# A recurrent block and an attention block on one core: preparing the weights beside the first chunk, fewer waits, single-pass bias rows, another order

## The chip, the cores and the metric

One NeuronCore of a Trainium2 chip runs the whole program. The metric is the device time of one execution in microseconds. The five engines are TensorE (PE), VectorE (DVE), ScalarE (ACT), GpSimd (POOL) and SyncE (SP), which here only issues transfers.

## What is computed

x is [2, 2048, 256] in float32 (2 sequences, 2048 positions, width 256). Two layers follow each other, each `x = x + s(xn) * silu(g(xn))` with `xn = layernorm(x)`:

```
layer 0: s = mamba block (in_proj 256->2x512, 4-tap causal conv, silu, dt = softplus(...),
             state scan h = exp(dt*A)*h + dt*B*x over 2048 positions, 512 channels x 16 states,
             y = sum_n h*C + D*x, gated by silu(z), out_proj) then layernorm and ffn 256->1024->256
         g = fp4_linear(silu(fp4_linear(x, w_gate)) * fp4_linear(x, w_up), w_down)   # blocks of 16, 704 wide
layer 1: s = attention over the 2 sequences at each position (16 heads of 16), with in and out projection
         g = three residual blocks of two 4-bit linears (weight q/7.5-1 times a scale per 16, plus
             a rank-32 part lora_b @ lora_a, plus bias) with layernorm and gelu between
```

The FP4 linears quantize both sides: `scale = max|block|/6`, rounding to the grid 0, 0.5, ... 6, and back.

## The kernel before, in words

The 2048 positions go in 16 chunks of 128 positions (TC) of both sequences. Everything is float32. One period of a software pipeline handles one chunk's state scan and, for chunks before and after it, the other steps. The steps have names, and each engine has its order of steps written out by hand (`PE_PLAN`, `ACT_PLAN`, `POOL_PLAN`, `DVE_PLAN`, `SP_PLAN`); a `+` or `-` behind a name says how many chunks ahead or behind the period's own chunk the step works. The engines meet only at semaphores, `at(name, chunk, k)`. PE's results outside the scan go through three PSUM banks in turn, in PE's own order (`BANK`, `EARLIER`): a step waits until the bank's user three steps before has been read.

The state scan goes by state n = 0..15 in two halves (a, b) of 4 x 128 columns: ACT's `exp` (L742) writes the decays into one of three PSUM tiles `unit`; POOL's `drive` (L965) multiplies wx = dt*x by the row B, broadcast to all partitions by a transfer `rows` of SP, and L971 adds the carry from the chunk before; DVE's `scan` (L1127), then `hc` (L1133), times the row C, then `clr` (L1140); ACT's `out` (L750) saves the carry; PE's `sum` (L537) transposes and adds hc into `y_ps`.

The front of a chunk is: DVE `f` (statistics), POOL `f`, ACT `xn`, `xhf`, PE `uT`, ACT `u`, PE `xi0..3` and `z0`, `z1`, ACT `tap0..3`, DVE `conv0`, `conv1`, ACT `xc0`, `xc1`, PE `xp` (L575), SP `wr` (rows B and C to DRAM), PE and ACT `dt0`, `dt1`, ACT `dtexp` (L813), `dtln`, POOL `log` (L1013), DVE `dt` (L1166), `wx` (L1170). POOL's `arg` and `fix0` make the first column's carry.

Six linears of a period end in a bias row (`bias_row`, L516): b0a, b1a, b2a, q and ao over 512 columns, v1 over 256. It is a product of a column of the identity, broadcast, with the six rows of `b_rows`.

Before this loop a block of its own prepares the weights, with memory that is given back afterwards. SP issues 34 loads on one semaphore, and PE, ACT, DVE and POOL wait for all of them. DVE (L196 to L202) finds the scales of the gate, up and down weights, POOL divides (L311), DVE rounds in four steps (L334 to L341), POOL multiplies back (L314), one weight after the other. DVE dequantizes the 4-bit weights (L343, L347). PE then makes 26 groups of transposes (L384), copied by ACT (L369), through three banks, and 12 folds (L396, L398): two products with the identity that turn a 4-bit weight and one that adds the low-rank part; ACT copies each (L372). The loop's block starts after all engines have left this one.

## Time and profile before

| | us |
|---|---|
| median of 3 runs | 1854.18 (1853.78 to 1857.8) |
| the profiled execution's own time | 1856.52 |
| its span, first to last instruction | 1854.7 |
| mean granted TensorE clock, share of full | 0.953 |
| PE, DVE, ACT, POOL busy | 1577.4, 1551.4, 1437.5, 1252.4 |

The profile is of one execution. Busy is the time in which an engine has an instruction running; an idle engine is only a loss where it is what the end waits for. Times in the rows are in microseconds from the first instruction, mean durations in ns.

### The profile page before, as it was taken

Reading aid. Unit: us, or ns where it says so; the run is one execution under the profiler, and the core shown is the slowest. Engines: PE = TensorE matmul, PEld = TensorE weight load, DVE = VectorE, ACT = ScalarE, POOL = GpSimd, SP = SyncE. Lnnn points to the kernel's source line nnn. Section 1 sums busy time; section 2 is a strip of 40 time slices with the busy share of each in tenths; the row PEclk is TensorE's granted clock in tenths of the full one; section 3 lists DMA queues with packets and bytes.
Section 4 is the critical chain, followed back from the end, with each engine's and each line's share of the span. In section 5 each row is a group of like instructions: output and inputs, shape, how many; then the busy total and the mean of one; then the engine's idle time right before and its main releaser. Section 6 shows DMA issues by size and latency. Waiting matters only on the chain.

```text
span 1854.7 us, 28175 instructions
## 1 busy us (share of the span) xinstructions
PE 1577.4 (85%) x7632; PEld 1164.4 (63%) x7632; DVE 1551.4 (84%) x2882; ACT 1437.5 (78%) x3076; POOL 1252.4 (68%) x1313
## 2 busy tenths in 40 slices
PE   0083768899999999999989999999989999999875
PEld 0051556586767677776767676767667767767653
DVE  0623999999999999999999999999999999999811
ACT  0034678898989898989889888989888989888723
POOL 0304676777777786868687777778686868787522
PEclk9976789999999999999999999999999999999987
DMA  8000111111111111111111111111111211111100
GB/s 209 0 6 29 52 47 58 47 57 37 58 48 60 43 52 51 59 47 52 52 52 52 44 51 50 58 47 46 58 52 47 63 41 58 46 44 55 35 0 12
DMA packets 68395, 91.70 MB, mean 49 GB/s; under 512 B 15674, under 2 KB 34686, under 8 KB 68238
## 3 DMA queue, kind: packets, MB, share of 16 engines
q1 hardware_dynamic: 68238, 89.91, 15.8%
q8 instruction: 62, 1.02, 0.2%
q14 instruction: 95, 0.78, 0.1%
HBM read 85.17 MB, written 4.72 MB: 48 GB/s over the span
## 4 chain that ended last, share of the span: by engine, by line
PE 27%; POOL 20%; DVE 16%; issue 16%; ACT 12%; POOLq 0%; ACTq 0%; DVEq 0%; DMA 0%
PE bank L511 10%; POOL drive L965 10%; PE bank L627 6%; DVE unit L1127 4%; DVE hc L1133 3%; PE bank L516 2%; PE y_ps L537 2%; ACT unit L742 2%; PE bank L498 1%; PE bank L563 1%; ACT op_a L709 1%; DVE xc L1158 1%; ACT L709 1%; ACT L923 1%; POOL s L1068 1%
## 5 line engine op out<-in xcount | busy, mean ns | idle before, releaser
L965 POOL TENSOR_TENSOR drive<-wx,rows 128x1024 f32<-128x1024 f32 x256 | 604.1, 2360 | 163.3 <-DVE unit L1127 82.8
L1127 DVE TENSOR_TENSOR_SCAN unit<-unit,drive 128x512 f32<-128x512 f32 x512 | 616.7, 1221 | 30.7 <-POOL drive L971 23.4
L742 ACT ACTIVATE unit<-dt,aneg 128x254 f32<-128x254 f32 x1024 | 441.9, 468 | 19.8 <-ACT carry L750 0.7
L1133 DVE TENSOR_TENSOR hc<-unit,rows 128x512 f32<-128x512 f32 x512 | 340.9, 684 | 8.8 <-issue 3.0
L537 PE MATMUL y_ps<-ident,hc 128*128 128x128 f32 x2048 | 278.1, 282 | 52.5 <-DVE hc L1133 52.4
L537 PEld LDWEIGHTS y_ps<-ident,hc 128*128 128x128 f32 x2048 | 241.2, 145 | 115.3 <-DVE hc L1133 71.8
L742 ACT ACT_TABLE_LOAD x109 | 139.8, 1283 | 3.7
L750 ACT ACTIVATE carry<-unit 128x4 f32<-128x4 f32 x512 | 79.3, 169 | 66.8 <-DVE unit L1140 63.0
L627 PE MATMUL bank<-op_a,w_f 128*128 128x256 f32 x512 | 115.7, 385 | 11.2 <-ACT op_a L709 11.2
L709 ACT ACT_TABLE_LOAD x77 | 98.8, 1283 | 22.4 <-PE bank L498 21.6
L511 PE MATMUL bank<-w_f,wide 128*128 128x256 f32 x512 | 113.3, 379 | 1.5 <-ACT wide L709 1.5
L627 PEld LDWEIGHTS bank<-op_a,w_f 128*128 128x128 f32 x512 | 97.0, 192 | 27.1 <-ACT op_a L709 11.9
L511 PE MATMUL bank<-w_d,hq_t 128*128 128x256 f32 (+1 forms) x384 | 109.3, 436 | 0.0
L511 PEld LDWEIGHTS bank<-w_f,wide 128*128 128x128 f32 x512 | 96.0, 190 | 14.9 <-ACT wide L709 1.7
L516 PE MATMUL bank<-b_rows,ident 6*128 6x512 f32 (+1 forms) x192 | 100.9, 605 | 0.0
L511 PEld LDWEIGHTS bank<-w_d,hq_t 128*128 128x128 f32 (+1 forms) x384 | 78.6, 219 | 27.0 <-issue 16.4
L593 PE MATMUL bank<-w_g,xq_t 128*128 128x352 f32 x256 | 87.3, 464 | 5.0 <-ACT xq_t L821 5.0
L1013 POOL TENSOR_SCALAR wide<-wx 128x1024 f32<-128x1024 f32 x16 | 58.4, 3652 | 46.8 <-ACT wx L813 46.8
L384 PE MATMUL bank<-ident,gate_raw 88*128 88x88 f32 x32 | 4.9, 355 | 97.2 <-POOL down_raw L314 97.2
L593 PE MATMUL bank<-w_u,xq_t 128*128 128x352 f32 x256 | 84.0, 460 | 1.3 <-ACT hq L827 1.1
L1038 POOL TENSOR_TENSOR hq<-q,j_scl 128x704 f32<-128x704 f32 x32 | 44.4, 1387 | 54.1 <-DVE q L1114 54.1
L722 ACT ACTIVATE xht<-bank,b_sm 128x256 f32<-128x256 f32 x96 | 48.7, 558 | 38.2 <-POOL b_sm L953 38.2
(220 smaller groups left out, 3439.4 us busy)
## 6 DMA issues: line engine op xcount, KB each, us to landing
rows<-rows_scratch SPq DMA_DIRECT2D x256, 256.0 KB, 3.3
x_t<-in_L_attn_x_dram SPq DMA_DIRECT2D x16, 256.0 KB, 3.7
x<-in_L_attn_x_dram SPq DMA_DIRECT2D x16, 256.0 KB, 3.3
out_dram<-x SPq DMA_DIRECT2D x16, 256.0 KB, 2.1
w_f<-in_L_attn_ffn_w_dram SPq DMA_DIRECT2D x2, 1024.0 KB
q_raw<-in_L_ffn_qweights_dram SPq DMA_DIRECT2D x1, 1536.0 KB
w_in<-in_L_attn_in_proj_w_dram SPq DMA_DIRECT2D x1, 1024.0 KB
qkv_raw<-attn_in_proj_weight_dram SPq DMA_DIRECT2D x1, 768.0 KB
```

What stands on the lines that cost most here:

```text
L511: last = t.matmul(dst[:, j * D:(j + 1) * D], lhs(k, j), rhs(k), start=(k == 0 and j == 0), stop=(stop and k == kp - 1), skip_group_check=True)
L516: return t.matmul(dst[:, 0:wide_ * D], ident[0:NROW, row:row + 1].to_broadcast([NROW, P]), b_rows[:, None, :].to_broadcast([NROW, wide_, D ...
L537: last = t.matmul(y_ps[j][:, g * P:(g + 1) * P], hc[n % NPROD][:, g * B + j, :], ident[:, :], start=False, stop=(n == NS - 1), is_transpos ...
L593: last = t.matmul(dst[:, 0:IH], xq_t[:, k, j, :], wt[:, k, half * IH:(half + 1) * IH], start=(k == 0), stop=(k == KD - 1))
L627: last = t.matmul(dst[:, a * TOK:(a + 1) * TOK], w_f1[:, k, (2 * m + a) * P:(2 * m + a + 1) * P], op_a[:, k, :], start=(k == 0 and a == 0) ...
L709: last = a_.activation(dst(k), src[:, k * TOK:(k + 1) * TOK], func, scale=scale(k), bias=bias(k))
L742: last = a_.activation(u[:, k * TOK:(k + 1) * TOK].rearrange("p (b t) -> p b t", b=B)[:, :, 1:TC], dt[p][:, g, :].rearrange("p (b t) -> p ...
L750: a_.activation(carry[:, n, 4 * half:4 * half + 4], unit_of(ch, n, half)[:, :].rearrange("p (s t) -> p s t", t=TC)[:, :, TC - 1], ACT.Copy)\
L965: g_.tensor_tensor(drive[n % 2][:, :, :].rearrange("p (g b) t -> p g b t", b=B), wx[p][:, :, :].rearrange("p g (b t) -> p g b t", b=B), ro ...
L1013: g_.tensor_scalar(tmp_u, wx[p][:, :, :], 1.0, -1.0, ALU.add, ALU.add).then_inc(S["sp_pool"], 1)
L1127: v.tensor_tensor_scan(u[:, :], u[:, :], d, 0.0, ALU.mult, ALU.add).then_inc(S["scan_done"], 1)
L1133: v.tensor_tensor(hc[n % NPROD][:, 4 * half:4 * half + 4, :].rearrange("p (g b) t -> p g b t", b=B), unit_of(ch, n, half)[:, :].rearrange( ...
```

## The change

1. Preparation and front together. The separate block is gone. In one block each engine does the front of chunk 0 (`FRONT`) between its preparation steps, and the loop leaves those steps out (`due`). Loads have four semaphores: `front_in`, `gate_in`, `lora_in`, `rest_in`. Raw weights lie in tiles that the loop uses later (drive, hc, rows, ops, xs, hx, hq), which is why those tiles are now allocated together. The groups of transposes and the folds use the two `y_ps` tiles in turn, not three banks, in the order low-rank, folds, rest, gate, down. The identity products of a fold are marked `is_transpose`.
2. Waits. `exp` waits for dt_ready, `out` and `drive` for carry_in, `drive` for wx_ready and `scan` for drive_ready only where the value first matters; `hc` b no longer waits for y_summed, `hc` no longer for its rows.
3. Bias rows. `b_rows` is loaded twice, at partitions 0 and 32. `b_two` holds the value rounded to float32r at 0 and what rounding left at 32; `pick` is two 32 x 32 identities. The bias row is one product of 64 partitions in float32r.
4. Order. The five plans have the same steps in another order. The period's boundary is moved, so some steps carry another offset (z1, sum7, aexp, v1, out10b, dt1, dtexp, hc15b and most of SP's); no step is added or dropped.

```diff
 ACT_PLAN = """
-    exp12a- hq1- hq2- out11a- exp12b- out11b- h1-- exp13a- ctx-- out12a- out12b- exp13b- out13a- exp14a- exp14b-
-    usave dtln gatec--- out13b- exp15a- out14a- exp15b- first out14b- exp0a b1n-- gatem- b1g-- out15a- exp0b
-    out15b- s1-- yg0- xq exp1a out0a out0b exp1b yg1- exp2a out1a exp2b g00 out1b g01 exp3a out2a exp3b g10
...
+    aexp-- dt1 out10b- v1-- dtexp out11a- exp12a- exp12b- h1-- hq1- out11b- ctx-- exp13a- dtln out12a- exp13b-
+    usave out12b- exp14a- out13a- out13b- hq2- first exp14b- out14a- exp15a- exp15b- b1n-- out14b- exp0a
+    gatec--- out15a- gatem- b1g-- exp0b s1-- out15b- xq exp1a yg0- yg1- out0a exp1b out0b exp2a out1a exp2b g00
...
 SP_PLAN = """
-    rows8- rows11- load+ rows10- rows12- rows13- wr rows14- rows15- rows0 rows1 rows3 rows2 store--- rows4
-    again- rows6 rows5 rows9 rows7
+    wr- rows0- rows15-- rows14-- rows2- rows1- rows3- rows4- store---- rows5- rows7- rows6- rows9- again--
+    rows8- rows10- load+ rows12- rows11- rows13-
 """
+FRONT = {
+    "SP": ("load", "wr"),
+    "POOL": ("f", "log"),
+    "ACT": ("xn", "xhf", "u", "tap0", "tap1", "z0", "tap2", "tap3", "z1", "xc0", "xc1", "usave", "xp", "dt0", "dt1",
+            "dtexp", "dtln"),
+    "PE": ("uT", "xi0", "xi1", "z0", "xi2", "xi3", "z1", "xp", "dt0", "dt1"),
+    "DVE": ("f", "conv0", "conv1", "dt", "wx"),
+}
             def bias_row(dst, row, wide_):
-                return t.matmul(dst[:, 0:wide_ * D], ident[0:NROW, row:row + 1].to_broadcast([NROW, P]),
-                                b_rows[:, None, :].to_broadcast([NROW, wide_, D]), start=False, stop=True,
+                return t.matmul(dst[:, 0:wide_ * D], pick[:, row:row + 1].to_broadcast([2 * LOW, P]),
+                                b_two[:, None, :].to_broadcast([2 * LOW, wide_, D]), start=False, stop=True,
                                 skip_group_check=True)
...
-                dve.wait_ge(*at("drive_ready", ch, 2 * n + 2))
+                if half == 0:
+                    dve.wait_ge(*at("drive_ready", ch, 2 * n + 2))
                 dve.wait_ge(*at("decay_ready", ch, 2 * n + half + 1))
...
+                    sp_step(sp, "load", 0)
+                    for dst, src in load_front:
+                        sp.dma_start(dst, src).then_inc(front_in, 16)
+                    for dst, src in load_gate:
+                        sp.dma_start(dst, src).then_inc(gate_in, 16)
+                    for dst, src in load_lora:
+                        sp.dma_start(dst, src).then_inc(lora_in, 16)
+                    for dst, src in load_rest:
+                        sp.dma_start(dst, src).then_inc(rest_in, 16)
+                sp_step(sp, "wr", 0)
+                sp.wait_ge(w_rounded, 4 * len(weights))
+                sp.wait_ge(turn_out, N_LB + N_FOLD)
...
+                pool_step(pool, "f", 0)
+                divide(0)
+                divide(1)
+                unscale(0)
+                divide(2)
+                unscale(1)
+                pool_step(pool, "log", 0)
+                unscale(2)
+                pool.wait_ge(rest_in, 16 * len(load_rest))
+                pool.wait_ge(turn_out, N_TURNS - IK)
...
+                act.wait_ge(front_in, 16 * len(load_front))
+                for name in FRONT["ACT"][:FRONT["ACT"].index("xp")]:
+                    act_step(act, name, 0)
+                nc.scalar.activation(aneg[:, :, :], al_raw[:, :, :], ACT.Exp).then_inc(neg_exp, 1)
+                for n, (dst, parts) in enumerate(lb_turns):
+                    turn_copy(dst, parts, n)
+                for name in FRONT["ACT"][FRONT["ACT"].index("xp"):]:
+                    act_step(act, name, 0)
...
+                pe.wait_ge(lora_deq, 2)
+                pe.wait_ge(turn_out, N_LB)
+                for n, (i, k) in enumerate(folds):
+                    m = N_LB + n
+                    pe.wait_ge(turn_out, m - 1)
+                    dst = y_ps[m % 2]
+                    for j in range(KD):
+                        nc.tensor.matmul(dst[:, j * P:(j + 1) * P], l_raw[:, i * KD + j, k * P:(k + 1) * P],
+                                         ident[:, :], start=(j == 0), stop=False, is_transpose=True, skip_group_check=True)
...
+                pe.wait_ge(w_out_done, 3)
+                for n, (dst, parts) in enumerate(gate_turns):
+                    turn_in(parts, N_LB + N_FOLD + N_REST + n)
+                pe.wait_ge(turn_out, N_TURNS)
...
+                dve_step(dve, "f", 0)
+                dve.wait_ge(gate_in, 16 * len(load_gate))
+                scale(0)
+                scale(1)
+                dve_step(dve, "conv0", 0)
+                step_of(0)
+                dve_step(dve, "conv1", 0)
+                round_(0)
+                scale(2)
+                step_of(1)
+                round_(1)
+                dve.wait_ge(lora_in, 16 * len(load_lora))
...
+                step_of(2)
+                round_(2)
+                dve_step(dve, "dt", 0)
+                dve_step(dve, "wx", 0)
...
+                dve.wait_ge(turn_out, N_TURNS - IK)
```

`scale` is the four instructions L196 to L202, `step_of` the first two and `round_` the last two of the rounding, `divide` and `unscale` POOL's two products. `load_front` holds w_in and nine transfers of columns and of the dt and B/C weights, `load_gate` three, `load_lora` four, `load_rest` the other 21.

## Rows read from the trace of the kernel before

**Rows 1.** The page: busy time by engine, and the row loads' time to landing.
```profile
PE 1577.4 (85%) x7632; PEld 1164.4 (63%) x7632; DVE 1551.4 (84%) x2882; ACT 1437.5 (78%) x3076; POOL 1252.4 (68%) x1313
...
rows<-rows_scratch SPq DMA_DIRECT2D x256, 256.0 KB, 3.3
```
**Rows 2.** Windows: length, busy time of each engine, granted clock, DMA share, GB/s.
```profile
0.00:10.00 10.00, 0.00 (x0) 0.00 (x0) 0.00 (x0) 1.28 (x1) 0.80 (x9) 1.00 0.87 274
10.00:20.00 10.00, 0.00 (x0) 0.00 (x0) 0.00 (x0) 0.00 (x0) 0.00 (x0) 1.00 0.80 162
45.00:100.30 55.30, 3.07 (x21) 3.10 (x22) 36.47 (x26) 2.10 (x5) 21.30 (x6) 1.00 0.00 0
...
109.40:136.00 26.60, 25.48 (x72) 15.79 (x72) 0.12 (x3) 4.61 (x12) 0.25 (x2) 0.55 0.00 1
...
400.00:500.00 100.00, 93.72 (x472) 69.26 (x470) 94.74 (x182) 89.33 (x192) 76.83 (x81) 1.00 0.15 51
900.00:1000.00 100.00, 93.72 (x471) 69.28 (x470) 94.32 (x179) 89.27 (x192) 76.86 (x81) 1.00 0.17 52
```
**Rows 3.** Timeline of the preparation: start, length, engine, line, operation.
```profile
45.27 2.28 DVE L196 TENSOR_REDUCE q_amax<-gate_raw 88x128 f32<-88x2048 f32 x1 [45.27 <-DMA lb_raw<-in_L_ffn_lora_b_dram]
...
49.20 3.67 POOL L311 TENSOR_TENSOR gate_raw<-gate_raw,q_rcp 88x2048 f32<-88x2048 f32 x1 [47.64 <-DVE q_rcp L202]
...
55.42 2.29 DVE L339 TENSOR_TENSOR gate_raw<-gate_raw,qt 88x2048 f32<-88x2048 f32 x1
...
94.68 5.62 DVE L347 TENSOR_TENSOR l_raw<-l_raw,sc_raw 128x3072 f32<-128x3072 f32 x1
...
99.26 0.46 ACT L369 ACTIVATE w_g<-bank 128x352 f32<-128x352 f32 x1
...
110.68 0.71 PE L396 MATMUL bank<-ident,l_raw 128*128 128x128 f32 x4
...
127.95 1.22 PE L396 MATMUL bank<-ident,l_raw 128*128 128x128 f32 x4
...
130.25 1.22 PE L396 MATMUL bank<-ident,l_raw 128*128 128x128 f32 x4
...
134.96 0.38 ACT L372 ACTIVATE w_l<-bank 128x256 f32<-128x256 f32 x1 [1.92 <-PE bank L398]
```
**Rows 4.** Timeline of chunk 0's front, to the first drive.
```profile
156.72 1.27 DVE L1158 SCALAR_TENSOR_TENSOR xc<-bank,cw,xc 128x256 f32<-128x256 f32 x3 [0.41 <-ACT xc L776]
...
168.69 3.64 POOL L1013 TENSOR_SCALAR wide<-wx 128x1024 f32<-128x1024 f32 x1 [21.65 <-ACT wx L813]
...
177.28 1.23 DVE L1166 TENSOR_TENSOR dt<-wide 128x1024 f32<-128x1024 f32 x1 [17.56 <-POOL wide L1018]
...
181.11 2.79 POOL L965 TENSOR_TENSOR drive<-wx,rows 128x1024 f32<-128x1024 f32 x1
```
**Rows 5.** The chain of waits over one period: start, length, what.
```profile
912.15 0.70 DVE s L1205
...
934.50 1.05 PE bank L516 x2
935.54 0.60 PE bank L498 x4
...
1000.61 1.05 PE bank L516 x2
...
1011.79 0.70 DVE s L1205
```
**Rows 6.** Groups by line, 912.15 to 1011.79: busy us, mean ns, idle before.
```profile
L1127 DVE TENSOR_TENSOR_SCAN unit<-unit,drive 128x512 f32<-128x512 f32 x32 | 38.5, 1221 | 1.9 <-POOL drive L971 1.7
L965 POOL TENSOR_TENSOR drive<-wx,rows 128x1024 f32<-128x1024 f32 x16 | 37.7, 2358 | 9.1 <-DMA rows<-rows_scratch 6.2 <-DVE unit L1127 2.9
...
L742 ACT ACT_TABLE_LOAD x7 | 9.0, 1283 | 0.2
...
L516 PE MATMUL bank<-b_rows,ident 6*128 6x512 f32 (+1 forms) x12 | 6.3, 603 | 0.0
```
**Rows 7.** The chain of waits in the tail.
```profile
1744.42 1.06 PE bank L516 x2
...
1755.06 0.44 PE bank L498 x4
```

More of the change, by code:

```diff
@@ L37 @@
 XW = NTAP - 1 + TC
+LOW = 32
 MAGIC = 1.5 * 2 ** 22
@@ L114, with due @@
 PERIODS = range(-6, NC + 6)
+FRONT = {
[6 more added lines that the diff above has]
+}
 def there(chunk):
     return 0 <= chunk < NC
-ORDER = [(_c + _o, _n) for _c in PERIODS for _n, _o in plan(PE_PLAN) if _n in USE and there(_c + _o)]
+def due(engine, name, chunk):
+    return there(chunk) and not (chunk == 0 and name in FRONT[engine])
+ORDER = [(0, _n) for _n in FRONT["PE"]]
+ORDER += [(_c + _o, _n) for _c in PERIODS for _n, _o in plan(PE_PLAN) if _n in USE and due("PE", _n, _c + _o)]
 BANK = {_key: _k % NBANK for _k, _key in enumerate(ORDER)}
@@ new lines, in program @@
+        folds = [(i, k) for i in range(NLIN) for k in range(KD)]
+        N_LB, N_FOLD, N_REST, N_GATE = len(lb_turns), len(folds), len(rest_turns), len(gate_turns)
+        N_TURNS = N_LB + N_FOLD + N_REST + N_GATE
+        weights = [(gate_raw[0].rearrange("p j (s b) -> p (j s) b", b=QB), GR, NGP * D // QB),
+                   (gate_raw[1].rearrange("p j (s b) -> p (j s) b", b=QB), GR, NGP * D // QB),
+                   (down_raw[:, :, :].rearrange("p k (s b) -> p (k s) b", b=QB), P, KD * IQ // QB)]
@@ L1276, in program, with pieces @@
+        def pieces(n):
+            rows_, nb = weights[n][1:]
+            return [small[n][0:rows_, 128 * i:128 * i + nb] for i in range(3)]
         with nc.Block() as block:
@@ L1313, in _, with scale, wait @@
             def _(dve):
-                for k in range(NUNIT):
-                    nc.vector.memset(unit[k][:, :].rearrange("p (s t) -> p s t", t=TC)[:, :, 0], 0.0).then_inc(c_prep, 1)
-                dve.wait_ge(c_prep, 6 * 3 + 3 + DG + NUNIT)
+                v = nc.vector
+                def scale(n):
+                    src, rows_, nb = weights[n]
+                    amax_, scl_, rcp_ = pieces(n)
+                    k = [4 * n]
+                    def wait():
+                        k[0] += 1
+                        dve.wait_ge(w_scaled, k[0])
+                    fp4_dve_scale(v, src, rows_, nb, amax_, scl_, rcp_, (w_scaled, 1), wait)
@@ L1318, in _ @@
+                for g in range(DG):
+                    v.tensor_scalar(d_diag[:, g, :], ident[:, :], dsk[:, g:g + 1], None, ALU.mult).then_inc(small_done, 1)
+                dve.wait_ge(turn_out, N_TURNS - IK)
                 for c in PERIODS:
                     for name, off in plan(DVE_PLAN):
-                        if there(c + off):
+                        if due("DVE", name, c + off):
                             dve_step(dve, name, c + off)
```

445 lines of the change are left out of this document (219 added, 226 removed).

## Prediction

> **What bounds the kernel now.** The page first: PE and DVE are both busy for over four fifths of the span, ACT and POOL for less [rows 1]. The windows then tell where the idle part is. Head: up to 45 us only loads run; from 45 to 100.3 the weights pass through DVE and POOL in turns, 36.5 us of DVE work in 55.3 us, with PE and ACT almost idle; then PE and ACT turn the weights and fold the low-rank parts until 136 [rows 2]. Only then is the first chunk of x loaded. Middle: a period is 99.64 us from one chunk's addition at L1205 to the next [rows 5], and in 100 us PE is busy for 93.7, DVE for 94.3, ACT for 89.3 and POOL for 76.9 [rows 2]. PE and DVE have some 6 us to spare, and the chain of waits changes engine all the time (it is on PE at 934.50 and 1000.61, on DVE at 912.15 [rows 5]), so what leaves one engine comes back only in part. Tail: behind the last chunk's scans, from about 1711 us, the chain of waits is mostly PE's [rows 7].
>
> The timeline of the head gives the anchors. All engines start at 45.27, when the last of all loads has landed; the dequantized low-rank weights are ready at 100.3; the second fold starts at 110.68, and the last fold's copy at 134.96 [rows 3]; x is asked for behind it. The front of chunk 0 then takes until 177.28 for dt, and the first drive, with which the state loop starts, is at 181.11 [rows 4]. This last is the head's length; what changes it shifts everything behind it by as much.
>
> **The head, part by part.** The load order is new: x and the ten transfers that the front needs, then the gate weights (2.1 MB), low-rank, rest. Up to the gate weights these are about 3.6 MB. The first 10 us moved 274 GB/s and the next ten 162, as there the small vector transfers are issued [rows 2]; 3.6 MB take 13 us by the first and 22 by the second. I take 18, since the six vector and column transfers of the front lie before the gate's. The upper bound for a mixing of the transfers is 33 us (15 more).
>
> DVE then sets the pace, because its order is one queue: statistics, then a wait for the gate weights, and behind that wait conv0. PE's xi2 needs the bank that conv0 frees, so the whole front is held until this wait ends; that costs the front some 10 us, but DVE is needed for the weights anyway. Up to the second dequantization step DVE has all of the 36.5 us [rows 2] less the last weight's stepping and rounding (1408 columns; by the 2.29 us of an addition of 2048 columns [rows 3] some 1.6 us each for two operations and, an estimate, half of that for the other two: 5 us), so 31.5, plus 5.1 us for conv0 and conv1 (12 steps, three in 1.27 us [rows 4]): 36.7 us. I add 2.5 us for conv1 waiting on PE and ACT. Dequantized at 18 + 36.7 + 2.5 = 57 us, where it was 100.3. DVE and POOL no longer alternate, since four waits on POOL (3.67 us each for the 2048 columns [rows 3]) lie beside other DVE work; if that cover were gone, the 14.7 us would return.
>
> POOL carries the divisions, the unscalings and log(1+.): 21.3 us [rows 2] plus 8.6 (log starts at 168.69 and lets dt go at 177.28 [rows 4]). It has log behind unscale(1), which waits for DVE's rounding at about 50 us, so log ends near 63 and dt near 65. Folds and turns end later than that, so it costs nothing.
>
> The folds wait for the dequantization. Before, each takes 2.30 us from start to start at the low clock (127.95 to 130.25), and its first half, four records for two identity products, 1.22 us there and 0.71 at the high clock [rows 3]. Marked as transposes they are two records, as the four transposes of a step are four records, in 0.60 us [rows 5]. I take 1.8 us: 12 x 1.8 = 21.6 us, end at 79; at the high clock, by 0.71 to 1.22, 12 x 1.05 puts it at 70. The clock stood at 0.55 on the mean in that stretch [rows 2] although PE hardly paused, so I take the low one. Then 6 turns of q/k/v and output weights and 8 of gate and up weights, on two PSUM tiles in place of three. A copy takes 0.46 us [rows 3]; with its hand-over, the clock low and one tile fewer I take 0.7: 14 x 0.7 = 9.8, end at 89. There POOL and DVE are let go, DVE has the scale of x (1.5 us), POOL its product; ACT has six more copies of w_down (3.6 us), then exp of the first column, then fix0. Drive0 at about 95.5. SP is held until the folds end, 79, and its row loads land in 3.3 us [rows 1], before the drives. The head thus goes from 181.1 to 95.5: **-85.6 us**; bounds 84 (high clock) and 110 (late loads), so -97 to -71.
>
> **The bias rows.** A period has 12 records at L516, 6.3 us of PE [rows 6]: five products of 512 columns and one of 256, two records each. On the chain a wide one costs 1.05 us [rows 5]. The trace of before has no float32r product. The nearest row is that of one-record products, the transposes: four of 128 columns, together 512, take 0.60 us on the chain [rows 5], 0.44 at best [rows 7]. Bounds: 0.44 from there, and 1.05 for no gain, by which 23.5 us of the sum below would be lost. The product is one record like theirs, so I take 0.44, a gain of 0.6. By the Trainium skill ("FP8 and Floating Point Precision", TensorE Precision Notes) true float32 is four passes through the array and reduced float32 one; an estimate from that page is 0.26 us for a wide row, a gain of 0.79, and no run shows it yet. In the period shown two wide rows lie on the chain, at 934.50 and at 1000.61 [rows 5]: 2 x 0.6 = **-1.2 us a period, 15 periods: -18 us**. In the tail the chain has nine of them, the first at 1744.42 [rows 7]: 9 x 0.6 = **-5.5 us**.
>
> **Leaner waits.** Per period they drop a wait from 31 exponentials, 30 carries, 29 drive steps, 16 scans and 48 in hc. DVE's idle time before scans is 1.9 us, of which 1.7 are for POOL's drive [rows 6], and that wait remains. The other 0.2 us, and as much again on hc and the carries, bound the gain at some 0.5 us a period, 7 us in all; a loss is excluded, as nothing is added. I take 0.
>
> **The order.** Steps and distances are nearly the same; aexp, v1, out10b, dt1, dtexp, z1 and sum7 cross the period's boundary only because it was moved, as do most of SP's. Counting changes of function around ACT_PLAN gives 20 table loads where the old plan has 19, at 1.28 us (seven of them are at L742 [rows 6]): +1.28 us on ACT, which goes from 89 to 90 busy and still has slack. SP's order changes which row load stands behind which hc wait; POOL waited 6.2 us a period for rows and 2.9 for scans [rows 6], and as POOL has 23 us to spare a shift of some us there is hidden. Net 0, from -2.3 us (DVE loses 3.5 of its 5.6 idle us, 1.2 of them counted already) to +2.5 us a period (the table load and as much again on the chain).
>
> **Sum**, against the profiled execution's own 1856.5: -85.6 - 18 - 5.5 = 1747.4. The median of the runs is 2.3 us lower, so **1745 us**.
>
> **Rivals.** (a) *PE's relief lets the period shrink.* DVE sets the floor at 94.0 us busy, and with some 3 us less PE work its waits on PE and on drives go too: 2.3 us a period more than summed, 35 us, 1710 us. For it: PE and DVE are both full. Against: the chain has ACT and POOL pieces as well. (b) *The order costs.* An extra table load on the chain plus as much waiting, 2.5 us x 15 = 37: 1782 us. For it: ACT is 89% busy already. (c) *Late loads.* Transfers issued later share the engines with the gate's, DVE starts 15 us later: 1760 us. For it: the 162 GB/s of 10 to 20 us. (d) *The other side: the clock.* With less PE work per period the granted clock, 1.00 in the middle windows [rows 2], falls to 1.2 GHz for part of each. Half a fold costs 1.22 against 0.71 us at the two levels [rows 3], so PE's 90 us become 90 x (1 + 0.7 s) for a share s. Head and tail give 91 us, 6.1 a period, so it decides from a period of 105.7, s = 0.25; at a third it would be 111 us and the kernel at 1854 - 91 + 15 x 11.4 = 1934. Against it: PE still idles only in pieces of a few us. The Trainium skill ("TensorE: Matmul & The Clock Gate", What's actually happening) has the throttled state as the default which activity releases; by that rule PE's lighter period would invite it. The trace agrees only in part: in the folds PE was busy for 25.5 of 26.6 us and the clock stood at 0.55 [rows 2]. (e) *The preparation stays serial:* DVE's wait for the gate weights holds the front and gains vanish. The sum of DVE work above speaks against it; even 30 us more leaves 1775.
>
> **Chances and range.** Forecast (1725 to 1765) 0.52; (a) 0.17; (b) 0.12; (c) and a mild (e), 1760 to 1775, 0.14; (d) 0.03; the rest 0.02. No more than 2 in 10 left out: 1707 to 1778. Faster 0.96, within 0.2% 0.01, slower 0.03; 0.2% is about what a measurement of this kernel can tell from none.
>
> **What would show it.** In the profile after: drive0 at 84 to 110 us; DVE's first reduce near 18; folds starting after 57, two transpose records and 1.8 us each; L516's successor with one record per row and under 0.6 us; the period between additions at L1205's successor 98.4 us; 20 table loads. The prediction is wrong if the dequantization ends after 75 us, or if the period moves by over 2 us either way.

## The result

The changed kernel takes 1798.52 us (median of 4 runs, 1796.36 to 1800.92), the kernel before 1855.99 beside it: ratio 0.9689, 95% interval 0.9668 to 0.9711. It is 3.1% faster, where the forecast of 1745 was 5.9% and the range ended at 1778.

The page of the profile after: its busy line, its clock line and two groups (line, engine, operation | busy us, mean ns | idle before):
```profile
PE 1568.4 (87%) x7512; PEld 1162.3 (65%) x7512; DVE 1556.0 (87%) x2887; ACT 1449.5 (81%) x3091; POOL 1246.3 (69%) x1314
...
PEclk8567898999999999999999998989999999999888
...
L959 DVE TENSOR_TENSOR_SCAN unit<-unit,drive 128x512 f32<-128x512 f32 x512 | 616.7, 1221 | 47.0 <-ACT unit L570 37.8
...
L579 ACT ACTIVATE carry<-unit 128x4 f32<-128x4 f32 x512 | 83.1, 169 | 138.3 <-DVE unit L973 137.8
```
The same two groups on the page of before:
```profile
L1127 DVE TENSOR_TENSOR_SCAN unit<-unit,drive 128x512 f32<-128x512 f32 x512 | 616.7, 1221 | 30.7 <-POOL drive L971 23.4 <-ACT unit L742 4.6 <-issue 0.2
...
L750 ACT ACTIVATE carry<-unit 128x4 f32<-128x4 f32 x512 | 79.3, 169 | 66.8 <-DVE unit L1140 63.0
```
DVE's busy time is 5 us above that of before [rows 1], with 60 us less span. What is new is in the idle column: scans (L959) wait for ACT's exponentials (L570) where they waited for POOL's drives, and ACT's carry copies (L579) stand 138 us waiting for DVE's clears (L973) where they stood 66.8.

I cut both spans at the first drive and at the first and the fifteenth addition of a chunk. The mark of an addition is L1205 before and L1038 after, the product with the gate just ahead of it:

| us | first drive | first addition | 14 periods | after them | span |
|---|---|---|---|---|---|
| before | 181.11 | 315.37 | 1393.42 | 145.91 | 1854.7 |
| after | 109.97 | 244.18 | 1411.46 | 138.86 | 1794.5 |
| change | -71.1 | -71.2 | **+18.0** | -7.1 | -60.2 |

The forecast had -85.6, then -16.8 (14 x 1.2), then -6.7 (the tail's 5.5 and the last period's 1.2). So 14 us are missing in the head and 35 in the middle. The windows of the 14 periods, after:
```profile
244.18:1655.64 1411.46, 1312.51 (x6452) 982.70 (x6451) 1309.61 (x2486) 1249.85 (x2666) 1060.74 (x1122) 0.96 0.16 50
```
and before:
```profile
315.37:1708.79 1393.42, 1317.75 (x6540) 977.09 (x6539) 1314.80 (x2484) 1238.09 (x2650) 1071.19 (x1123) 0.99 0.16 51
```
DVE has 5 us less work in them than before and ACT 12 more, so for DVE the periods grew by idle time. PE is busy for 5 us less only, although its bias rows alone went from 88.1 to 40.5 us in these periods: its other work takes 42 us more, at a granted clock of 0.96 for 0.99.

The head, timeline after, DVE (start, length, line, operation [idle before]):
```profile
28.20 2.28 DVE L217 TENSOR_REDUCE ctx<-drive 88x128 f32<-88x2048 f32 x1 [17.43 <-DMA hq<-in_L_ffn_w_down_dram]
30.52 0.22 DVE L219 TENSOR_SCALAR ctx<-ctx 88x128 f32<-88x128 f32 x1
...
34.21 1.61 DVE L219 TENSOR_SCALAR s<-s 88x128 f32<-88x128 f32 x1
...
56.10 3.49 DVE L1367 TENSOR_SCALAR rows<-rows 88x2048 f32<-88x2048 f32 x1
...
65.94 6.72 DVE L1395 TENSOR_TENSOR ops<-ops,v 128x3072 f32<-128x3072 f32 x1
...
82.88 3.53 DVE L999 TENSOR_TENSOR dt<-wide 128x1024 f32<-128x1024 f32 x1 [2.30 <-POOL wide L849]
...
104.28 0.69 DVE L217 TENSOR_REDUCE x_amax<-xn 128x32 f32<-128x512 f32 x1 [14.24 <-ACT w_u L1274]
```
and the queue of SP, PE and POOL in the same stretch:
```profile
6.83 0.44 SPq L1099 DMA_DIRECT2D x_t<-in_L_attn_x_dram  x1
...
72.71 0.69 PE L1325 MATMUL y_ps<-ident,ops 128*128 128x128 f32 x2 [15.11 <-DVE ops L1395]
73.33 1.22 PE L1327 MATMUL y_ps<-hx,xs 32*128 32x256 f32 x2
74.48 0.69 PE L1325 MATMUL y_ps<-ident,ops 128*128 128x128 f32 x2
...
93.92 3.02 PE L1306 MATMUL y_ps<-ident,hq_t 128*128 128x128 f32 x12
...
109.97 2.34 POOL L795 TENSOR_TENSOR drive<-wx,rows 128x1024 f32<-128x1024 f32 x1
```

| us | gate weights in | dequantized | folds end | turns end | first drive |
|---|---|---|---|---|---|
| forecast | 18 | 57 | 79 | 89 | 95.5 |
| measured | 28.2 | 72.7 | 93.9 | 104.3 | 110.0 |

All of the gap is there when the folds start: 10.2 us because the gate weights come later, the rest because DVE takes 44.5 us where I had 39.2. Behind that each stage is within 1 us of its term: 12 folds at 1.77 us, at the low clock (0.50), for 1.8. Windows over the folds, after:
```profile
72.00:94.00 22.00, 21.29 (x49) 9.52 (x50) 15.44 (x17) 4.22 (x11) 13.16 (x4) 0.50 0.00 1
```

The bias row, on the chain of waits after (start, length, what): a wide row at the high clock, a row of 256 columns at the high clock, and a wide row at the low clock.
```profile
803.72 0.42 PE bank L343
...
875.69 0.32 PE bank L343
...
1747.41 0.72 PE bank L343
```
A wide row at the high clock is one record of 0.42 to 0.44 us for 1.05 [rows 5]; the forecast took 0.44.

### The profile page after: what moved, and what is told of

Read it like the earlier page. It is cut to its first block, busy times and chain, and to the rows that moved or that the text cites. A ratio compares the mean times of both kernels' runs of the same rounds, so it can differ in the third digit from the quotient of the medians.

```text
span 1794.5 us, 26244 instructions
## 1 busy us (share of the span) xinstructions
PE 1568.4 (87%) x7512; PEld 1162.3 (65%) x7512; DVE 1556.0 (87%) x2887; ACT 1449.5 (81%) x3091; POOL 1246.3 (69%) x1314
## 4 chain that ended last, share of the span: by engine, by line
PE 46%; ACT 20%; DVE 14%; issue 12%; POOL 4%; DMA 2%; SPq 1%; POOLq 0%; ACTq 0%; DVEq 0%
PE bank L338 20%; PE bank L420 7%; PE bank L454 6%; DVE unit L959 5%; ACT unit L570 5%; PE y_ps L364 5%; PE bank L325 2%; DVE hc L966 2%; ACT L536 2%; POOL drive L795 2%; ACT L617 2%; ACT L570 2%; PE bank L343 1%; ACT ops L536 1%; PE bank L390 1%
## 5 line engine op out<-in xcount | busy, mean ns | idle before, releaser
L959 DVE TENSOR_TENSOR_SCAN unit<-unit,drive 128x512 f32<-128x512 f32 x512 | 616.7, 1221 | 47.0 <-ACT unit L570 37.8
L570 ACT ACTIVATE unit<-dt,aneg 128x254 f32<-128x254 f32 x1024 | 437.7, 467 | 7.7
L338 PE MATMUL bank<-w_l,ops 128*128 128x256 f32 x768 | 193.2, 396 | 20.2 <-ACT ops L536 18.6
L579 ACT ACTIVATE carry<-unit 128x4 f32<-128x4 f32 x512 | 83.1, 169 | 138.3 <-DVE unit L973 137.8
L338 PEld LDWEIGHTS bank<-w_l,ops 128*128 128x128 f32 x768 | 145.1, 196 | 60.4 <-issue 30.7
L338 PE MATMUL bank<-w_d,hq_t 128*128 128x256 f32 (+1 forms) x384 | 130.4, 500 | 23.4 <-ACT hq_t L668 23.4
L338 PEld LDWEIGHTS bank<-w_d,hq_t 128*128 128x128 f32 (+1 forms) x384 | 89.6, 248 | 62.6 <-ACT hq_t L668 24.9
L454 PE MATMUL bank<-ops,w_f 128*128 128x256 f32 x512 | 120.1, 388 | 2.3 <-DVE hq L1016 1.7
L338 PE MATMUL bank<-w_f,wide 128*128 128x256 f32 x512 | 113.3, 379 | 0.1
L536 ACT ACT_TABLE_LOAD x77 | 98.8, 1283 | 15.2 <-PE bank L325 14.0
L454 PEld LDWEIGHTS bank<-ops,w_f 128*128 128x128 f32 x512 | 94.9, 192 | 23.1 <-ACT ops L532 5.4
L338 PEld LDWEIGHTS bank<-w_f,wide 128*128 128x128 f32 x512 | 96.0, 190 | 12.9 <-ACT wide L536 0.3
L325 PE MATMUL bank<-ident,hx 128*128 128x128 f32 x448 | 68.5, 282 | 28.8 <-ACT hx L549 17.6
L390 PE MATMUL bank<-u_t,w_in 128*128 128x262 f32 x256 | 74.0, 417 | 16.1 <-DVE xc L994 11.7
L844 POOL TENSOR_SCALAR wide<-wx 128x1024 f32<-128x1024 f32 x16 | 62.9, 3934 | 35.9 <-ACT wx L642 35.9
```

The costliest lines, as they stand in the source:

```text
L325: last = t.transpose(dst[0:rows, n * P:(n + 1) * P], src, ident[:, :])
L338: last = t.matmul(dst[:, j * D:(j + 1) * D], lhs(k, j), rhs(k), start=(k == 0 and j == 0), stop=(stop and k == kp - 1), skip_group_check=True)
L390: last = t.matmul(dst[:, 0:B * XW], w_in[:, k, g * P:(g + 1) * P], u_t[:, k, :, :], start=(k == 0), stop=(k == KD - 1))
L454: last = t.matmul(dst[:, a * TOK:(a + 1) * TOK], w_f1[:, k, (2 * m + a) * P:(2 * m + a + 1) * P], op_a[:, k, :], start=(k == 0 and a == 0) ...
L536: last = a_.activation(dst(k), src[:, k * TOK:(k + 1) * TOK], func, scale=scale(k), bias=bias(k))
L570: last = a_.activation(u[:, k * TOK:(k + 1) * TOK].rearrange("p (b t) -> p b t", b=B)[:, :, 1:TC], dt[p][:, g, :].rearrange("p (b t) -> p ...
```

## The experiments

The kernels were timed in groups on several chips (after; e1 to e4; e5 to e8; e9 to e12; e13 to e16; e17 and e18), and those of a group share their runs of the kernel before. Ratios are to it, and differences between kernels are taken from the ratios, times 1856 us. The median of the kernel before moved from 1847.8 to 1856.0 us between the groups (in one of them its runs go from 1845.9 to 1864.2), so a difference across groups can be off by some us more than its intervals say. The columns "14 periods" and "first drive" are from each one's profile, and the clock is the mean granted in those periods.

| | ratio (95%) | median us | first drive | 14 periods, clock |
|---|---|---|---|---|
| before | 1 | 1855.99 | 181.1 | 1393.4, 0.99 |
| after | 0.9689 (0.9668 to 0.9711) | 1798.5 | 110.0 | 1411.5, 0.96 |
| e1_order_old | 0.9574 (0.9551 to 0.9597) | 1770.2 | 108.1 | 1386.3, 0.98 |
| e2_bias_old | 0.9806 (0.9784 to 0.9828) | 1814.2 | | 1418.1, 0.99 |
| e3_waits_old | 0.9766 (0.9741 to 0.9791) | 1807.4 | | 1417.9, 0.96 |
| e4_head_only | 0.9657 (0.9637 to 0.9677) | 1784.4 | 109.8 | 1393.5, 0.99 |
| e5_b_order_new | 1.0142 (1.0116 to 1.0168) | 1882.7 | 171.1 | 1431.9, 0.97 |
| e6_b_bias_new | 0.9911 (0.9888 to 0.9935) | 1838.7 | 171.8 | 1390.3, 0.98 |
| e7_load_now | 0.9684 (0.9658 to 0.9711) | 1795.5 | 104.5 | 1413.3, 0.96 |
| e8_b_waits_new | 1.0014 (0.9993 to 1.0034) | 1858.1 | 170.7 | 1393.8, 0.99 |
| e9_old_order_load_now | **0.9523 (0.9495 to 0.9550)** | 1765.5 | 102.8 | 1384.6, 0.99 |
| e10_hq2_early | 0.9684 (0.9656 to 0.9712) | 1795.7 | | 1407.8, 0.98 |
| e11_act_plan_old | 1.0434 (1.0401 to 1.0467) | 1934.3 | | 1535.7, 0.93 |
| e12_pe_plan_new | 0.9987 (0.9965 to 1.0009) | 1851.6 | | 1466.0, 0.99 |
| e13_one_silu_visit | 0.9903 (0.9875 to 0.9930) | 1833.0 | | 1444.7, 0.95 |
| e14_down_product_first | 0.9707 (0.9685 to 0.9729) | 1797.0 | | 1411.7, 0.96 |
| e15_both | 0.9920 (0.9895 to 0.9945) | 1836.3 | | 1442.5, 0.95 |
| e16_old_order_down_first | 0.9530 (0.9509 to 0.9552) | 1765.7 | | 1385.5, 0.97 |
| e17_exp_first | 0.9655 (0.9629 to 0.9681) | 1789.1 | 110.0 | 1407.9, 0.97 |
| e18_pool_products_cut | 0.9473 (0.9449 to 0.9496) | 1757.1 | 94.2 | 1383.6, 0.99 |

### The four parts, one by one

e1, e2 and e3 are the changed kernel with one part put back: the five plans (e1), the bias rows (e2), the waits (e3). e4 is the kernel before with the new head alone. e5, e6 and e8 are the kernel before with one part alone: the plans, the bias rows, the waits. The edits are the parts of the diff; for e2:
```diff
-                return t.matmul(dst[:, 0:wide_ * D], pick[:, row:row + 1].to_broadcast([2 * LOW, P]),
-                                b_two[:, None, :].to_broadcast([2 * LOW, wide_, D]), start=False, stop=True,
+                return t.matmul(dst[:, 0:wide_ * D], ident[0:NROW, row:row + 1].to_broadcast([NROW, P]),
+                                b_rows[0:NROW, None, :].to_broadcast([NROW, wide_, D]), start=False, stop=True,
```


> The changed kernel with the five plans of before (head, waits and bias rows stay new). Between the additions of the first and the 15th chunk the kernel before took 1393.4 us, the changed one 1411.5. Theory A, the new order costs: PE stands before the down product for hq2, its clock falls to the low level, and the long chain of PE work behind it runs slow. Then with the old order this stretch is 1375 to 1394 us, the whole about 1765 to 1780 us against 1798.5, and the granted clock in the middle windows is back at 0.98 to 1.00. Theory B, the cheaper bias rows leave PE less active and so the clock falls: then the stretch stays at 1405 to 1412 us, the clock at 0.95, the whole at 1790 to 1800.

> The changed kernel with the float32 bias rows of before (two records each, 1.05 us for a wide one on the chain, against 0.43 now). Theory A (order): the chain of the new order is PE's for more than half of a period, so dearer rows cost: 0.6 us for each of two to five rows a period, 18 to 45 us, 1816 to 1840 us. Theory B (activity): the clock returns to 0.98 or more and the whole falls to 1780 to 1790 us. If the rows are off the chain: within 4 us of 1798.5.

> The changed kernel with all waits of the state loop as before. My prediction gave the leaner waits 0 us, at most 0.5 us a period (7 us in all): 1798 to 1806 us. The rival, that each wait costs its engine some 50 ns of issue where instructions are short (154 waits a period over three engines), would give 2 us a period and more: 1830 us.

> The changed kernel with order, waits and bias rows of before: only the preparation beside the front is new. The head was 71.1 us shorter to the first drive, the tail's gain is the bias rows'. If the parts add up: 1856 - 71 = 1785 us, the stretch between the first and the 15th addition 1393 us. If the new head also disturbs the middle (its phase of the clock, the different tiles in memory), the stretch is longer than 1398 us.

> The kernel before with only the five new plans. Theory A (the order costs by itself): 1856 plus the stretch's 18 us plus what the float32 bias rows cost in the new order's PE chain, 1874 to 1900 us, the clock in the middle at 0.95 to 0.97. Theory C, the new order only pays together with the cheap bias rows and leaner waits it was made for: slower by the same, but then bias rows alone on the old order gain less than 10 us. If the order is neutral: 1850 to 1862.

> The kernel before with only the new bias rows. The prediction's own term: two wide rows on the chain a period, 1.2 us x 15 = 18 us, and 5.5 in the tail: 1832 us. If PE has slack there in the old order and DVE sets the pace: only the tail's 5 to 7 us, 1849. If PE's lighter period lets the clock fall (the rival of the prediction): slower than 1856.

> The kernel before with only the leaner waits. By the prediction 0 to 7 us of 1856; by the rival of 50 ns a wait some 30 us. Its middle stretch of 1393 us shows it, as nothing else differs.

**Head.** e4 is 64 us under the kernel before, and its periods have the length they had before. The profiles say 71 because in the profiled execution of before the first drive was at 181.1; in e5, e6 and e8, whose head is that of before, it was at 171.1, 171.8 and 170.7. The folds make the difference: in those three they ran at the high clock and took 14.6 us, in the profile of before 24.3 us at 0.55. Windows of e6:
```profile
110.00:124.00 14.00, 13.67 (x66) 8.95 (x66) 0.00 (x0) 4.02 (x11) 0.00 (x0) 1.00 0.01 1
```
With the new head they stood at 0.50 in all 16 profiled executions. Whether that comes from their marking as transposes or from PE's wait ahead of them (15.11 us in after, 0.55 before) no run tells apart.

**Bias rows.** Alone they take off 0.0089, 16.5 us (e6); from e4 to e1 it is 15.4 us, waits included, and from e2 to after 21.7, all within their intervals of each other. The forecast had 23.5. e6 came out between its two expectations, 1832 and 1849.

**Waits.** On the old order nothing (e8, +0.1%, the interval holds 1). On the new order with the new bias rows putting the waits back costs 14 us (e3; by the two intervals 8 to 20, by the medians 9), more than the 7 us that I had as the most. On the new order with the old bias rows they seem worth nothing: e5 less the head's gain (e4) gives 0.9799, and e2, which has the lean waits besides, 0.9806. So the gain isn't secured, and which wait it is I can't name.

**Order.** It costs: e1 is 21 us under after (15 to 27), and the new order alone adds 26 us to the kernel before (e5, 22 to 31). Two routes and one answer; by the medians it is 28 and 29.

Where it costs, one period each of e2 (new order) and e4 (old order), which differ in the order and in the waits and have the same bias rows. Groups by line, 850.99 to 952.52 of e2:
```profile
L959 DVE TENSOR_TENSOR_SCAN unit<-unit,drive 128x512 f32<-128x512 f32 x32 | 38.6, 1220 | 2.5 <-ACT unit L570 2.3
...
L579 ACT ACTIVATE carry<-unit 128x4 f32<-128x4 f32 x32 | 5.1, 167 | 7.4 <-DVE unit L973 7.4
...
L1028 DVE TENSOR_TENSOR sz<-y_ps,sz 128x512 f32<-128x512 f32 x2 | 1.3, 686 | 1.1 <-PE y_ps L364 1.1
...
L1038 DVE TENSOR_TENSOR s<-bank,ops 128x512 f32<-128x512 f32 x1 | 0.7, 691 | 0.9 <-PE bank L356 0.9
```
and 841.06 to 940.95 of e4:
```profile
L954 DVE TENSOR_TENSOR_SCAN unit<-unit,drive 128x512 f32<-128x512 f32 x32 | 38.6, 1221 | 1.9 <-POOL drive L798 1.7
...
L577 ACT ACTIVATE carry<-unit 128x4 f32<-128x4 f32 x32 | 4.9, 168 | 2.5 <-DVE unit L967 2.3
...
L1022 DVE TENSOR_TENSOR sz<-y_ps,sz 128x512 f32<-128x512 f32 x2 | 1.3, 682 | 0.0
```
The work is the same. In the new order the scans wait for exponentials instead of drives, the additions wait for PE (1.1 and 0.9 us), and ACT waits three times as long in front of carry copies. Two such waits, timeline of ACT in e2:
```profile
892.84 0.17 ACT L579 ACTIVATE carry<-unit 128x4 f32<-128x4 f32 x1 [0.22 <-DVE unit L973]
895.79 0.17 ACT L579 ACTIVATE carry<-unit 128x4 f32<-128x4 f32 x1 [2.78 <-DVE unit L973]
...
896.62 0.85 ACT L570 ACTIVATE unit<-dt,aneg 128x254 f32<-128x254 f32 x2
898.94 0.17 ACT L579 ACTIVATE carry<-unit 128x4 f32<-128x4 f32 x1 [1.47 <-DVE unit L973]
```
ACT stands for 2.8 us on clear 13b, which DVE does behind the product dt, and exponential 14b is queued behind it. These rows show where engines stand; which of the waits costs time is for the next runs.

### Is it one plan, or one place in a plan?

e11 is the changed kernel with the old ACT_PLAN alone, e12 is e9 with the new PE_PLAN alone.

> The changed kernel with only ACT_PLAN of before. It has 19 table loads a period instead of 20, and hq2 right behind hq1. If the loss sits in ACT's order (the extra load of 1.28 us and hq2): ratio 0.957 to 0.962, as with all five plans old. If it is in PE's or DVE's order: 0.966 or above.

> The kernel of e9 (old order, load at once) with only PE_PLAN of the change. If PE's order brings the loss, this is slower than e9 by 15 us or more (ratio 0.963 or above); if not, within 4 us of e9.

Both are far slower: e11 by 138 us than after, far beyond anything that I had in mind with "0.966 or above", and e12 by 86 us than e9. The plans of one set fit each other, and one can't be judged without the rest. Four repairs inside the new set followed. e10 moves one copy, `hq2`; e14 has that and the down product before `sum13`; e13 joins two groups of silu steps, so that the tables change 286 times where the changed kernel has 316; e16 is e9 with the down product first.
```diff
# e10: ACT_PLAN
-    ... ctx-- exp13a- dtln out12a- exp13b- usave out12b- exp14a- out13a- out13b- hq2- first exp14b-
+    ... ctx-- exp13a- hq2- dtln out12a- exp13b- usave out12b- exp14a- out13a- out13b- first exp14b-
# e13: ACT_PLAN
-    ... tap3+ xc0+ out7b exp9a out8a exp9b z1+ out8b xc1+ exp10a
+    ... tap3+ xc0+ out7b out8a z1+ out8b xc1+ exp9a exp9b exp10a
# e14, e16: PE_PLAN
-    ... sum12- sum13- dn- sum14-
+    ... sum12- dn- sum13- sum14-
```


> The changed kernel with one step moved: ACT copies the last part of the transposed h (hq2) before dtln instead of behind four exponentials and three carries. In the trace PE stood 1.8 us before the down product for it, and the clock fell around it. Theory A1 (this wait starts the slow stretch): the down product starts right behind sum13, 2 us earlier, 14 periods of it: 15 to 30 us less than the changed kernel, ratio 0.953 to 0.961. Theory A2 (the order costs in many places, dn stands behind sum13 anyway): within 5 us of it, ratio 0.966 to 0.972.

> The changed kernel, with ACT's exp9a and exp9b behind z1 and xc1 instead of between z0 and z1: the table goes to silu once there, not twice, so two table loads (2.56 us) leave ACT and, by the chain, the path from x1's addition to dt. Theory L (these loads on the chain are the order's cost): the period falls by 1.3 to 2.5 us, 18 to 36 us, ratio 0.950 to 0.959. Theory G (the order is bound by PE from the down product to x1, 56 us without a gap, and the loads are beside it): less than 5 us, 0.966 to 0.971. If the delayed exp9 starves DVE's scans: slower, above 0.972.

> The changed kernel, with hq2 early and PE's down product in front of sum13, so that PE does it while DVE makes hc13, for which it stood 1.9 us, and for hq2 1.8 us more. Theory G: PE's long stretch starts 3.7 us earlier, its clock does not fall in it, the period goes to 98 to 99 us: ratio 0.948 to 0.958. Theory L: under 5 us. If the sum that comes 5.9 us later holds up hc15 and DVE: slower than 0.9689.

> The kernel of e9 (old order, load at once) with the down product in front of sum13. In its trace PE stands 2.5 us for hc13 right ahead of the down product, whose parts are ready. If that wait is on the loop of the period: 1 to 2.5 us a period, ratio 0.932 to 0.945. If DVE with 93.8 us busy of 98.6 sets the pace: 0.950 to 0.954. If the late sum13 holds DVE: above 0.956.

None gains. e13 is the telling miss: 30 table loads fewer, at 1.28 us 38 us of ACT work, and the kernel is 40 us slower than after. (With e14's edits besides, e15, it gave 0.9920.) Its edit also moves exponentials 9a and 9b back, and in its profile the scans wait 69.6 us for exponentials, after 37.8. So fewer table loads don't help where exponentials come later for them; what the new order's 15 additional loads cost by themselves isn't shown. Nor does the scans' wait for exponentials measure the loss: in e10 and e14 it is 58.2 and 61.6 us, and both are as fast as after.

e17 goes for the waits shown above:
```diff
# ACT_PLAN
-    ... out10b- v1-- dtexp out11a- exp12a- exp12b-
+    ... out10b- exp12a- v1-- dtexp out11a- exp12b-
-    ... out13a- out13b- hq2- first exp14b-
+    ... out13a- hq2- first exp14b- out13b-
# DVE_PLAN
-    ... hc13b dt+ clr13b scan14a
+    ... hc13b clr13b dt+ scan14a
```


> The changed kernel with three moves inside its new order: the exponential 12a before the copy of v1, the exponential 14b before the carry copy 13b, and DVE's clear 13b before the product dt. In a period of the new order ACT stands idle 7.4 us in front of carry copies, waiting for DVE's clears (2.5 us in the old order), 2.8 us of it for clear 13b behind the product dt and 1.5 us for clear 14a, and DVE then waits 3.0 us for exponentials (0.2 us in the old order). If the new order loses by exponentials that stand behind waiting carry copies, the carry copies' idle time falls by over 2 us a period and the period by 1 to 1.5 us: ratio 0.957 to 0.963, as far as the old order. If the loss is spread over the whole order and another wait takes the place of this one, the ratio stays at 0.967 to 0.971, and ACT's idle time at the carries falls alone.

The page of e17:
```profile
L579 ACT ACTIVATE carry<-unit 128x4 f32<-128x4 f32 x512 | 82.3, 167 | 89.5 <-DVE unit L973 89.0
...
L959 DVE TENSOR_TENSOR_SCAN unit<-unit,drive 128x512 f32<-128x512 f32 x512 | 616.7, 1221 | 56.4 <-ACT unit L570 45.9 <-POOL drive L802 6.4
```
The carry copies' wait falls by 49 us, 3 us a period where the theory asked for over 2, and yet the period falls by 0.3 us and not by 1 to 1.5; the scans' wait for exponentials rises from 37.8 to 45.9. The ratio, 0.9655, lies between the two expectations and 0.003 under after, about as much as the two intervals can tell. It is nearer to the rival: one wait took the place of another.

### The head's two terms

e7 and e9 load x at once, in place of the step whose wait on a preset POOL meets late:
```diff
-                    sp_step(sp, "load", 0)
+                    sp.dma_start(x_t[:, :, :], xv[0]).then_inc(S["x_loaded"], 16)
```


> The changed kernel, but the first chunk's load is issued without the step's wait. In the changed kernel SP issues its first transfer at 6.83 us, after POOL has raised some seventy semaphores, because the step waits for the preset of uT_full; before, the first load was issued at 0.72. If that wait carries through: everything in the head 5 to 6 us earlier, 1793 us against 1798.5. If the loads are bound by the transfers: under 2 us.

> The changed kernel with the old order and the first load issued at once: the two edits that were faster than the changed kernel by themselves (0.9574 and 0.9684 of before against 0.9689). If they add: head 5 us shorter, ratio about 0.954 to 0.957, some 1765 us. If the clock phase decides more than the 5 us: 0.957 or above.

The first drive comes 5.5 and 5.3 us sooner, so a good half of the 10.2 us was SP standing until 6.83 (in e9 the gate weights are in at 22.35). In the time e7 gains 1 us against after, inside the intervals, and its 14 periods took 1.8 more. e9, all but the new order, is with e16 the fastest whole kernel measured: 31 us under after. Against e1 it gains 9.5 us by the ratios, more than the 5 expected, and 4.7 by the medians.

e18 is e9 with POOL's products over the three weights cut to one block of 16 columns each; it leaves out the scaling of all other blocks:
```diff
-                    nc.gpsimd.tensor_tensor(src, src, pieces(n)[2][:, :, None].to_broadcast([rows_, nb, QB]), ALU.mult)\
+                    nc.gpsimd.tensor_tensor(src[:, 0:1, :], src[:, 0:1, :], pieces(n)[2][:, 0:1, None].to_broadcast([rows_, 1, QB]),
```


> The old order with the first load at once (as e9_old_order_load_now), but POOL's two products over each of the gate, up and down weights are cut to one block of 16 columns; this leaves out the division by the scales and the multiplication by them for the other blocks. DVE has all its work. If DVE's preparation takes 44.5 us where 39.2 were forecast because POOL works at the same time, its four-column-block products and the product dt go back to 0.22, 1.22 and 1.22 us (1.61, 2.56 and 3.49 us in the changed kernel) and the dequantization ends 4 to 6 us earlier after the first reduction, drive0 4 to 8 us earlier: ratio 0.948 to 0.951. If the lengthening comes from something else (the transfers that still land), they keep their length and the ratio stays at 0.951 to 0.953.

Two of POOL's products and DVE in e9, timeline:
```profile
26.21 3.68 POOL L1227 TENSOR_TENSOR drive<-drive,ctx 88x2048 f32<-88x2048 f32 x1 [10.72 <-DVE ctx L223]
...
28.36 1.61 DVE L219 TENSOR_SCALAR s<-s 88x128 f32<-88x128 f32 x1
...
33.49 2.56 DVE L1365 TENSOR_SCALAR rows<-drive 88x2048 int32<-88x2048 int32 x1
...
49.16 3.50 POOL L1227 TENSOR_TENSOR hq<-hq,xq_t 128x1408 f32<-128x1408 f32 x1 [1.12 <-DVE xq_t L223]
...
50.25 3.49 DVE L1367 TENSOR_SCALAR rows<-rows 88x2048 f32<-88x2048 f32 x1
...
60.09 6.72 DVE L1395 TENSOR_TENSOR ops<-ops,v 128x3072 f32<-128x3072 f32 x1
```
and the same four of DVE in e18:
```profile
28.38 0.22 DVE L219 TENSOR_SCALAR s<-s 88x128 f32<-88x128 f32 x1
...
32.11 1.21 DVE L1365 TENSOR_SCALAR rows<-drive 88x2048 int32<-88x2048 int32 x1
...
46.65 1.22 DVE L1367 TENSOR_SCALAR rows<-rows 88x2048 f32<-88x2048 f32 x1
...
54.22 4.25 DVE L1395 TENSOR_TENSOR ops<-ops,v 128x3072 f32<-128x3072 f32 x1
```
From the first reduction to the folds' release it is 44.5 us in e9 and 36.1 in e18. DVE is busy for 43.9 of the 44.5 us and nowhere waits for POOL in them, so it isn't a wait that e18 took away: the instructions got shorter. The theory holds and was too small: 8.4 us, not 5, are lost to POOL working beside DVE.

## Why the prediction was right or wrong

Against the profile of before the forecast had 109.1 us and 60.2 came. Of the 49 us between them the order is 25 (the 14 periods of after against those of e1, 1411.5 and 1386.3), the head 14.5, and the bias rows 9.5 (7.3 us for 16.8 in the 14 periods).

**The head: mechanism right, two terms mis-sized.** DVE's queue sets the pace, then the folds at the low clock, then the turns, as forecast. "I take 18" for the gate weights measured 28.2, inside the bound of 33; 5.3 to 5.5 us of it are SP's wait for a preset, a wait that I had not looked for. DVE's 39.2 us measured 44.5, since I took every duration from a stretch in which DVE and POOL alternate: beside POOL they are longer (e18). The sum was 95.5 against 110.0, at the bound given for late loads. That the folds would run at the low clock came true, but on thin ground: I read it off one execution of the old head, and in the three profiled later its folds ran at 1.00. The same execution also flattered the gain: its head was 10 us longer than theirs.

**The bias rows: price right, count too high.** 0.44 was forecast and 0.42 to 0.44 measured. In the undisturbed periods of e1 and e9 the period is 98.5 to 98.8 us (the forecast said 98.4), against mostly 99.6 to 99.9 in e4, so 1.1 us for the 1.2 forecast. But four of the 14 periods of e1 take 100.0 us or more and eat half of it: 1393.5 less 1386.3 is 7.3 us for 14 periods. The profiled execution of e1 is the slowest of its five, and by the ratios 15.4 to 21.7 of the 23.5 us came, so half is the low end. Behind the periods it gives 3.3 us (e4 146.0, e1 142.6), where the forecast had 6.7; one of the nine rows counted there is the narrow one (0.64 us at 1809.02 on the chain of before), for which 0.6 us were too much. After has 7.1 there with the new order.

**The waits: right on the old order.** e8 is within its interval of nothing. On the new order e3 puts them at 8 to 20 us, above the bound of 7, and the pair of e5 and e2 at nothing.

**The order: the failed step.** "Net 0, from -2.3 us to +2.5 us a period": it costs 21 to 26 us, 1.4 to 1.8 us a period. That alone takes 1745 to 1766 or 1771, out of the forecast's 20 us on either side but not out of the range, which ended at 1778; it took the head's two terms and the bias rows besides. The 1.4 to 1.8 us lay inside the bounds given for the order, and rival (b), 2.5 us a period, has the sign and almost the size, but its mechanism is not shown: the 20th table load is real (316 in all against 301), yet no run prices it by itself, and e13, with 30 loads fewer, was slower. What I did not do was to follow each exponential through the two plans: I counted steps and distances ("nearly the same") and gave ACT's slack as cover. The traces show that this cover fails: with 10 us of slack a period on ACT the scans wait for exponentials (37.8 us in all, 4.6 before), and ACT stands in front of carry copies. That these waits are what the order costs is argued and not shown, since e10 and e14 have more of the first and e17 has less of the second at the length of after. Which moves of the plans make the loss stays open: no single plan could be exchanged, four local repairs gained nothing, and e17 shifted the wait.

**Rivals.** (a) The usual period never went below 98.5, so PE's relief gave nothing beyond the sum. (c) holds in part: late loads were 10.2 us of the 14.5, over half of them SP's wait and not the transfers. (d) The clock: in after it stands at 0.96 over the 14 periods, and the longer a period, the lower its clock (99.7 us at 0.98, 101.6 at 0.95, 103.1 at 0.93). Windows of the longest one, 1047.84 to 1150.93:
```profile
1047.84:1090.00 42.16, 38.07 (x182) 26.13 (x180) 38.40 (x80) 39.30 (x81) 30.20 (x28) 0.96 0.13 40
1090.00:1130.00 40.00, 37.37 (x181) 28.76 (x182) 35.12 (x60) 31.65 (x71) 31.89 (x40) 0.87 0.18 53
1130.00:1150.93 20.93, 20.93 (x103) 17.09 (x102) 20.17 (x42) 18.72 (x42) 14.10 (x14) 1.00 0.19 62
```
and its chain of waits:
```profile
1092.93 0.38 ACT hq_t L667
1093.32 0.27 ACT hq_t L668
1093.59 0.14 issue
1093.72 10.56 PE bank L338 x24
...
1150.03 0.87 PE bank L356 x2
...
1150.93 0.70 DVE s L1038
```
The down product (L338, 24 records) stands behind ACT's copies of hq_t and takes 10.56 us; over the 14 periods of after it begins when PE has idled 0.8 to 2.9 us and takes 7.6 us or more. In e14 and e17, where PE doesn't idle there, it takes 5.93 us (but for e17's first), yet e14's 14 periods are as long as after's (1411.7) and their clock is 0.96 again: the low spell lies elsewhere. So the order costs without the clock: e2 has the new order, 0.99 and periods of mostly 101.0 to 101.6 us, against 99.6 to 99.9 in e4. But (d) holds in a mild form besides. From e2 to after the bias rows take 47.6 us of work off PE, and the clock goes from 0.99 to 0.96; the rest of PE's work gets 32 us longer. In after the six periods at 0.97 and more take 99.8 us on the mean and the eight at 0.95 and less 101.6. If the clock makes that difference, it is 14 us in all, an estimate and no more, since e10, at 0.98, is only 3.6 us shorter over its 14 periods. A low spell can stretch a period of the new order, since PE is 46% of its chain (27% before), and it costs nothing where others set the pace: in the kernel before a period at 0.98 is as long as one at 1.00. The Trainium skill ("TensorE: Matmul & The Clock Gate", What's actually happening) says that activity releases the throttled state. The down product agrees with it in part: at full speed without idle time in e14, low behind idle time in after, but also up to 8.0 us without any in the kernel before, and at full speed behind 1.5 to 2.2 us of it in six periods of e2. The folds don't agree: they kept 0.50 over 22 us with PE busy for 21.29 of them. (e) did not come.

## What to carry to other kernels

Before a new order of steps is costed at nothing, time it alone; e5 is that run. On paper, follow the producer with the fewest buffers (here exponentials, three tiles) through both orders and ask of each what is queued in front of it, since an engine's mean slack doesn't exclude waits there. Judge a repair by the length of the period and not by the wait that it removes: here e10, e14 and e17 shortened or removed theirs, and the period hardly moved. When work of DVE and POOL that took turns is laid side by side, don't take the durations from the serial stretch. Time the parts of a change apart: this one hid a loss of 1.2 to 1.4% behind a gain of 4.3% (e1).

## What the runs showed of the hardware

- Some of DVE's instructions grow beside POOL's products: 88 x 128 from 0.22 to 1.61 us, 88 x 2048 from 1.22 to 3.49, 128 x 3072 with two inputs from 4.25 to 6.72, and POOL's own `wide` product (L844) from 3.64 (e18) to 6.74 us (e9). The Trainium skill ("Trainium Architecture — The Big Picture", What this means for kernel authors) has the port pair that DVE and GpSimd share as an exclusive lock. The trace agrees as far as it goes: each growth, 1.3 to 2.5 us, is less than one product of POOL (3.67 us), e18 shows that it goes with POOL's work, and what grew ends when POOL's product has ended or about its own length later: in e9 the 88 x 128 at 29.97 behind POOL's end at 29.89, the 88 x 2048 at 53.74 behind 52.66. Not every instruction takes part: the reduction over 88 x 2048 at 26.05 takes 2.27 us beside POOL's product at 26.21, and 2.28 in e18.
- A float32r bias row takes 0.42 us for 512 columns and 0.32 for 256 on the chain at the high clock: by these two, an estimate of 0.4 ns a column and some 0.2 us whatever the width. The Trainium skill ("FP8 and Floating Point Precision", TensorE Precision Notes) has four passes for true float32 and has reduced float32 cut to the array's own precision; that this is one pass was my reading of it. The estimate of 0.26 us, a quarter of 1.05, is 0.16 us below the measured row.
- ACT's 301 table loads before and 316 after took 1.283 us each, and the next instruction of ACT started right behind (0.01 us, the median).
- Dropping some 154 waits a period from three engines changed nothing on the old order: ratio 1.0014 (0.9993 to 1.0034, e8).
